# Attention values weighed in four column tiles of 32, softmax sums taken apart, x's parts in two homes

## The reference, cut to what matters

```python
q, k, v = wq @ xf, wk @ xf, wv @ xf            # 32 channels each, per image
att = softmax(einsum('bmi,bmj->bij', k, q), axis=2)
x = x + wo @ einsum('bij,bmj->bmi', att, v)    # attention 1
t = tokens(x)                                  # (4, 1024, 64)
u = layernorm(t); t = t + softmax(u @ u.T) @ u # attention 2
w = layernorm(t)                               # 8 experts, the best two by router
t = t + sum_of_two(p_k * (w @ expert_k + bias_k))
```

## Time and profile before

| | us |
|---|---|
| median of 3 executions | 223.43 (223.21 to 224.67) |
| the profiled execution's own time | 224.33 |
| its span, first to last instruction | 222.6 |
| TensorE busy | 206.3 |
| VectorE busy | 143.4 |
| ScalarE busy | 107.6 |
| GpSimd busy | 62.5 |

### The profile page before, as it was taken

One profiled execution on the slowest core, in us unless ns is written; L12 is line 12 of the kernel. 1 busy time (PEld: TensorE's weight loads), 2 busy tenths in 40 slices (PEclk: granted clock), 3 DMA queues, 4 the chain that ended last, 5 costly groups with the idle time before them and its releaser, 6 DMA issues.

```text
span 222.6 us, 2932 instructions
## 1 busy us (share of the span) xinstructions
PE 206.3 (93%) x1075; PEld 105.1 (47%) x1075; DVE 143.4 (64%) x358; ACT 107.6 (48%) x166; POOL 62.5 (28%) x75
## 2 busy tenths in 40 slices
PE   7899899969989989999999999899999999998993
PEld 2454443543643434643543445334445343477773
DVE  2589865776334898168189665836775282798970
ACT  2630664283675476564654544765645567201110
POOL 8230000044040030003001268730177751017260
PEclk9999999996999999999999999999999999999999
DMA  4661000000000000000000000020000002000021
GB/s 105 145 148 43 3 0 0 0 1 0 3 1 0 0 0 3 0 0 0 3 0 1 0 3 1 0 47 0 3 0 0 0 3 49 0 0 3 0 47 47
DMA packets 3341, 3.67 MB, mean 16 GB/s; under 512 B 2176, under 2 KB 2432, under 8 KB 3328
## 3 DMA queue, kind: packets, MB, share of 16 engines
q1 hardware_dynamic: 3328, 3.50, 6.9%
HBM read 2.45 MB, written 1.05 MB: 16 GB/s over the span
## 4 chain that ended last, share of the span: by engine, by line
PE 67%; DVE 18%; ACT 5%; POOL 4%; issue 2%; DMA 1%; SPq 1%; DVEq 0%; POOLq 0%
PE acc L490 22%; DVE rowmax L1107 7%; PE ring L551 6%; PE ring L596 6%; PE ring L552 5%; PE ring L465 4%; PE ring L483 4%; PE acc L626 3%; POOL sm L368 3%; PE ring L443 2%; PE ring L454 2%; PE ring L455 2%; PE ring L444 2%; DVE stats L1140 1%; DVE tok L1186 1%
## 5 line engine op out<-in xcount | busy, mean ns | idle before, releaser
L902 ACT ACTIVATE prob<-ring,shift 128x1024 f32<-128x1024 f32 x32 | 35.6, 1112 | 27.6 <-PE ring L552 27.5
L1107 DVE TENSOR_REDUCE rowmax<-ring 128x1 f32<-128x1024 f32 x32 | 37.9, 1219 | 15.6 <-PE ring L465 15.4
L899 ACT ACTIVATE prob<-ring 128x1024 f32<-128x1024 f32 x32 | 32.1, 1024 | 20.1 <-PE ring L483 19.9
L368 POOL TENSOR_TENSOR sm<-sm,minus_half 128x8 f32<-128x8 f32 x8 | 15.8, 1975 | 85.4 <-DVE sm L1150 85.4
L490 PE MATMUL acc<-prob,val 128*64 128x512 f32 x128 | 32.0, 622 | 0.0
L490 PE MATMUL acc<-prob,u 128*64 128x512 f32 x128 | 31.0, 606 | 0.0
L1246 DVE TENSOR_TENSOR prod<-ring,gate 128x1024 f32<-128x1024 f32 x16 | 19.4, 1221 | 9.3 <-PE ring L596 8.8
L551 PE MATMUL ring<-zst 128*128 128x512 f16 x64 | 24.5, 383 | 0.4 <-DVE rowmax L1107 0.4
L552 PE MATMUL ring<-zsw,zst 128*128 128x512 f16 x64 | 24.3, 379 | 0.0
L483 PE MATMUL ring<-kst,qst 98*128 98x512 f32 x64 | 21.4, 425 | 2.2 <-ACT prob L899 0.9
L465 PE MATMUL ring<-qst,kst 96*128 96x512 f32 x64 | 22.4, 436 | 0.6 <-DVE rowmax L1107 0.4
(11 more groups left out here) (155 smaller groups left out, 311.0 us busy)
## 6 DMA issues: line engine op xcount, KB each, us to landing
xin<-in_x SPq DMA_DIRECT2D x8, 256.0 KB, 3.9
out<-ob SPq DMA_DIRECT2D x6, 128.0 KB, 2.3
e_in<-in_L_ffn_expert_w SPq DMA_DIRECT2D x2, 128.0 KB
out<-ob SPq DMA_DIRECT2D x4, 64.0 KB, 2.0
eb_in<-in_L_ffn_expert_b SPq DMA_DIRECT2D x8, 2.0 KB
wo<-in_L_conv_wo SPq DMA_DIRECT2D x2, 8.0 KB, 2.4
r_in<-in_L_ffn_router_w SPq DMA_DIRECT2D x2, 2.0 KB
w<-in_L_conv_wq SPq DMA_DIRECT2D x1, 16.0 KB, 3.5
```

Of the source, the lines that this page charges most:

```text
L368: pool.tensor_tensor(sm[:, 3, :], sm[:, 2, :], minus_half[:, :], ALU.pow).then_inc(s_rs, 1)
L899: act.activation(prob1[:, j % DEEP, :], flat(filled(act, f"st{j}", b)), ACT.Exp).then_inc(s_p1, 1)
L902: act.activation(prob2[:, j % DEEP, :], flat(filled(act, f"s{j}", b)), ACT.Exp, bias=shift[:, :], accum_out=rsum2[b % 2][:, j:j + 1]).then ...
L1107: dve.tensor_reduce(rowmax[:, tile:tile + 1], flat(filled(dve, f"mx{tile}", b)), AX.X, ALU.max).then_inc(s_mx, 1)
```

## The change

- Values are weighed in four column tiles of 32, each with a quarter of the 1024 columns; the ones column in the stationary tile is gone, and with it the padding to 64.
- For images 0 and 1 the softmax sums are matmuls of their own: `sum1` multiplies the same `prob1` by a tile of ones, after each pair of weighings. `project_out` picks them with a small matmul.
- For images 2 and 3 ScalarE takes them: `sum_row` reads the maxima's scores in the ring buffer, once `row_max` (which now gives the negative maximum) is done, and writes their exp in place with an accumulated sum. Only then is the buffer released.
- `xst` has two homes. `round_x(2)` and `round_x(3)` move into the exps of image 0, `split_x(3)` ahead of the first `rstd`.
- Image 1's `project_v` and `values` move ahead of image 0's `max_row`; `split_k(1)` ahead of it too; the fillers of `keep_clock` there are 4 instead of 3 + 3.
- `wo4` is one load and waits for nothing. `project_out` has two matmuls over 256 columns instead of four over 130. `eb_blk` is made later.

The core of the diff (index changes of `xst` and renumbered waits are mostly left out; blank lines too):

```diff
 DEEP = 4
+QUARTER = N // 4
+BY_ROWS = (2, 3)
...
-HEAD = [("w3", 0), ("q", 0), ("k", 0), ("vx", 0)] + per_tile("mx", 0) + [("q", 1), ("k", 1), ("mr", 0)]
+HEAD = [("w3", 0), ("q", 0), ("k", 0), ("vx", 0)] + per_tile("mx", 0) + [("q", 1), ("k", 1), ("vx", 1), ("mr", 0)]
...
 FIRST = [("st0", 0), ("st1", 0), ("mx0", 1), ("st2", 0), ("mx1", 1), ("st3", 0), ("mx2", 1), ("mx3", 1), ("st4", 0),
-         ("mx4", 1), ("st5", 0), ("mx5", 1), ("st6", 0), ("mx6", 1), ("st7", 0), ("mx7", 1), ("vx", 1), ("mr", 1),
-         ("po", 0)]
+         ("mx4", 1), ("st5", 0), ("mx5", 1), ("st6", 0), ("mx6", 1), ("st7", 0), ("mx7", 1), ("mr", 1), ("po", 0)]
...
         wo4 = sb("wo4", [C, 4, M])
+        ones = sb("ones", [P, M])
...
         vx2 = sb("vx2", [P, M + C], F32R)
-        wo_blk = sb("wo_blk", [P, 2, C + 1])
+        wo_blk = sb("wo_blk", [P, 4, C])
+        pick = sb("pick", [P, 4])
...
-        xst = sb("xst", [P, N], F32R)
+        xst = two("xst", [P, N], F32R)
...
         kst = two("kst", [P, N], F32R)
-        val = two("val", [P, T, C])
+        val = two("val", [P, T, M])
...
         rinv1 = sb("rinv1", [P, T])
+        rsum1 = two("rsum1", [P, T])
...
                 return table[name]
+            if name[:-1] == "mx" and b in BY_ROWS:
+                return s_row, T * BY_ROWS.index(b) + int(name[-1]) + 1
...
                 sp.dma_start(w3[n * M:(n + 1) * M, :, :], w.unsqueeze(1).to_broadcast([M, 2, C])).then_inc(s_w3, 16)
-            sp.wait_ge(s_const, 1)
-            for h in range(2):
-                sp.dma_start(wo4[:, 2 * h, :], wo).then_inc(s_wol, 16)
+            sp.dma_start(wo4[:, :, :], wo.unsqueeze(1).to_broadcast([C, 4, M])).then_inc(s_wol, 16)
...
         def _(pool):
-            pool.memset(wo4[:, :, :], 0.0).then_inc(s_const, 1)
+            pool.memset(ones[:, :], 1.0).then_inc(s_const, 1)
...
                                pattern=[[-1, P]], channel_multiplier=1).then_inc(s_const, 1)
-            pool.memset(nmax[:, :, :].bitcast(F32), 0.0)
-            for home in range(2):
-                pool.memset(val[home][:, :, M + 1:C], 0.0)
-                pool.memset(val[home][:, :, ONE:ONE + 1], 1.0).then_inc(s_pool, 1)
+            pool.memset(nmax[:, :, :].bitcast(F32), 0.0).then_inc(s_pool, 1)
+            pool.wait_ge(s_pool, 2)
+            pool.memset(qst[0][ROW:ROW + 2, :].bitcast(F32), 1.0).then_inc(s_pool, 1)
             pool.wait_ge(s_pool, 3)
-            pool.memset(qst[0][ROW:ROW + 2, :].bitcast(F32), 1.0).then_inc(s_pool, 1)
-            pool.wait_ge(s_pool, 4)
...
             pool.wait_ge(s_const, 3)
+            pool.memset(pick[:, :], 0.0)
...
             pool.memset(tile_mask[:, :], 1.0).then_inc(s_pool, 1)
-            pool.wait_ge(s_pool, 5)
+            pool.wait_ge(s_pool, 4)
...
                                pattern=[[-E, T]], channel_multiplier=1).then_inc(s_pool, 1)
-            pool.wait_ge(s_pool, 6)
+            pool.wait_ge(s_pool, 5)
...
                 pool.wait_ge(s_xr, b + 2)
-                first = xst[C:P, :]
+                first = xst[b % 2][C:P, :]
...
             split_x(2)
+            split_x(3)
             rstd(0, s_ve1, s_rs1, sm1)
-            split_x(3)
...
                         pe.wait_ge(s_xs, h + 1)
-                    rows = xst[:, h * CHUNK:(h + 1) * CHUNK]
+                    rows = xst[b % 2][:, h * CHUNK:(h + 1) * CHUNK]
...
+            def quarter(b, j, q):
+                return prob1[:, j % DEEP, :].rearrange("p (h q n) -> p q h n", h=2, q=4)[:, q]
...
                     pe.wait_ge(s_gbs, 1)
-                weigh(acc1, val[b % 2], prob1, j, s_p1, s_av1, b)
+                pe.wait_ge(s_p1, T * b + j + 1)
+                for q in range(4):
+                    mm = pe.matmul(acc1[q * M:(q + 1) * M, 0:QUARTER], val[b % 2][:, j, :], quarter(b, j, q),
+                                   start=(j == 0), stop=(b in BY_ROWS and j == T - 1))
+                if b in BY_ROWS and j == T - 1:
+                    mm.then_inc(s_av1, 1)
+            def sum1(b, j):
+                for q in range(4):
+                    mm = pe.matmul(acc1[q * M:(q + 1) * M, QUARTER:2 * QUARTER], ones[:, :], quarter(b, j, q),
+                                   start=False, stop=(j == T - 1))
+                if j == T - 1:
+                    mm.then_inc(s_av1, 1)
...
                 weigh1(b, j + 1)
+                if b not in BY_ROWS:
+                    sum1(b, j)
+                    sum1(b, j + 1)
...
                 if b == 0:
-                    pe.wait_ge(s_wblk, 2)
-                for t in range(4):
-                    o = (t % 2) * 2 * (C + 1)
-                    mm = pe.matmul(buf[:, t // 2, o:o + 2 * (C + 1)], agg[:, t * P:(t + 1) * P],
-                                   wo_blk[:, :, :].rearrange("p h c -> p (h c)"), start=True, stop=True)
+                    pe.wait_ge(s_wblk, 4)
+                for h in range(2):
+                    mm = pe.matmul(buf[:, h, 0:4 * C], agg[:, h * P:(h + 1) * P],
+                                   wo_blk[:, :, :].rearrange("p q c -> p (q c)"), start=True, stop=True)
+                    if b not in BY_ROWS:
+                        mm = pe.matmul(buf[:, h, 4 * C:4 * C + 4], agg[:, QUARTER + h * P:QUARTER + (h + 1) * P],
+                                       pick[:, :], start=True, stop=True)
...
                     keep_clock(2)
-            pe.wait_ge(s_wol, 2 * 16)
+            pe.wait_ge(s_wol, 16)
...
             project_qk("k", 1)
-            keep_clock(3)
+            project_v(1)
             max_row(0)
-            keep_clock(3)
+            keep_clock(4)
...
             weigh_pair1(0, 6)
-            project_v(1)
...
                 act.wait_ge(s_x[b], 32)
-                act.activation(xst[:, :], xin[:, b, :], ACT.Copy).then_inc(s_xr, 1)
+                act.activation(xst[b % 2][:, :], xin[:, b, :], ACT.Copy).then_inc(s_xr, 1)
...
+            def sum_row(b, tile):
+                buf = flat(filled(act, f"mx{tile}", b))
+                act.wait_ge(s_mx, T * b + tile + 1)
+                act.activation(buf, buf, ACT.Exp, bias=rowmax[:, tile:tile + 1],
+                               accum_out=rsum1[b % 2][:, tile:tile + 1]).then_inc(s_row, 1)
...
                 act.wait_ge(s_av1, b + 1)
-                act.activation(agg[:, :], acc1[:, :], ACT.Copy).then_inc(s_agg, 1)
+                width = QUARTER if b in BY_ROWS else CHUNK
+                act.activation(agg[:, 0:width], acc1[:, 0:width], ACT.Copy).then_inc(s_agg, 1)
...
             for h in range(2):
-                act.activation(xst[:, chunk(h)], xin[:, 0, chunk(h)], ACT.Copy).then_inc(s_xr, 1)
+                act.activation(xst[0][:, chunk(h)], xin[:, 0, chunk(h)], ACT.Copy).then_inc(s_xr, 1)
...
                     act.activation(dst[0:ROW, chunk(h)], ring[0:ROW, k, h, :], ACT.Copy).then_inc(s_rounded, 1)
-            act.wait_ge(s_const, 3)
...
             round_k(1)
+            values(1)
...
-            for j in range(4):
+            for j in range(3):
                 exp1(0, j)
+            round_x(2)
+            exp1(0, 3)
...
                 act.activation(r_blk[rows, h, 0, :], r_in[rows, :], ACT.Copy).then_inc(s_er, 1)
-            for j in range(4, T):
-                exp1(0, j)
+            exp1(0, 4)
+            exp1(0, 5)
+            round_x(3)
+            exp1(0, 6)
+            exp1(0, 7)
             copy_agg(0)
-            values(1)
             max_row(1)
-            round_x(2)
...
             values(2)
-            round_x(3)
...
             exp1(1, 6)
+            sum_row(2, 0)
             exp1(1, 7)
+            sum_row(2, 1)
...
             exp2(0, 0)
+            sum_row(2, 2)
...
             exp2(0, 1)
+            sum_row(2, 3)
             exp2(0, 2)
+            sum_row(2, 4)
...
             exp2(0, 3)
+            sum_row(2, 5)
...
             exp2(0, 4)
+            sum_row(2, 6)
...
             exp2(0, 6)
+            sum_row(2, 7)
...
             max_row(2)
+            sum_row(3, 0)
...
             exp1(2, 0)
-            for j in range(1, 6):
-                exp1(2, j)
+            sum_row(3, 1)
+            exp1(2, 1)
+            exp1(2, 2)
+            sum_row(3, 2)
+            exp1(2, 3)
+            exp1(2, 4)
+            sum_row(3, 3)
+            exp1(2, 5)
...
             gap_exp(0)
 
+            sum_row(3, 4)
             exp2(1, 0)
...
             exp2(1, 1)
+            sum_row(3, 5)
...
             exp2(1, 3)
+            sum_row(3, 6)
...
             stack_swapped(2)
+            sum_row(3, 7)
...
             def row_max(b, tile):
-                dve.tensor_reduce(rowmax[:, tile:tile + 1], flat(filled(dve, f"mx{tile}", b)), AX.X, ALU.max).then_inc(s_mx, 1)
+                dve.tensor_reduce(rowmax[:, tile:tile + 1], flat(filled(dve, f"mx{tile}", b)), AX.X, ALU.max,
+                                  negate=True).then_inc(s_mx, 1)
...
                 rm = rowmax[:, :].unsqueeze(2)
```

(41 more changed lines are left out.)

9 lines of the change are left out of this document (5 added, 4 removed).

## The result

The changed kernel takes 232.78 us (median of 4 executions, 231.34 to 234.13); before, 223.55 in the same round. The ratio is 1.039, 95% interval 1.0347 to 1.0433: slower by 9.2 us. The profiled execution took 233.8 us, its span is 232.1.

What follows compares the result with a forecast made beforehand. It took TensorE, busy 206.3 of 222.6 us, as the bound. 222.6 - 4.9 - 0.9 + 7.45 + 1.55 - 1.3 made 224.5; that +1.9 on the median 223.43 gave 225.4 us, range 218.5 to 229.0.

Steps and rivals of the forecast that it cites:

- a rival of one stretch at one place, 82 to 87: TensorE idles 3.9 of 5.3 us, the clock drops, some 1.5 us of work doubled: 226.9; shared chance 0.26.
- the cost of the change to ones: Switching from values to ones in the weighings costs 0.15 us each time, giving 226.6; shared chance 0.26.
- the walk through the queues: Following the code's order with profiled durations, from 50.2 us, adding stall to stall: 224.5 in all.
- the lead of 5.8 us out of the first stage: Maxima of image 2 (mx1(2)) start at 60.5 us, 5.8 ahead of before.
- Four column tiles: Weighing in full overlap: 1.0 us a pair for images 2 and 3, 1.87 with sums for images 0 and 1.
- x in two homes: First stage: q(2) no longer waits for x(2)'s split, 4.9 us won with moved values; exp1(1,5) another 0.9.
- Values moved ahead: Image 1's values projection leaves the first stage's end, where 1.8 us goes; scores1(1,0) comes 0.9 us earlier.
- The dearest place: From 77.85 to 87.6 us, ScalarE's queue behind sum_row(2,5): a lead of 4.2 us becomes 1.65 behind.
- Image 3's sums: sum_row(3,4) and sum_row(3,5) hold exps behind them, costing 1.2 and 1.0 us; then 3.2 behind.
- The norm chain swallows the won weighing: Won 0.86 us of weigh(2,0) and (2,2), and image 3's (3,0) and (3,2), vanish in waits for VectorE and GpSimd.
- The rival of waits that catch up: From 60.5 us, VectorE and ScalarE run ahead while TensorE stands; half of 11.6 us regained: 219.6; chance 0.28.
- Four tiles not side by side: In the weighings four column tiles run two at a time, 13.8 us more: 242; chance 0.10.

Runs made afterwards that it cites:

- b_fillers: Changed kernel with 39 unused filler matmuls put where TensorE waits, the last six held until VectorE has read attention 2's result: 227.74 us, ratio 1.0176.
- f_rows_image2: Changed kernel with ScalarE row sums for image 2 alone, image 3's sums taken by ones on TensorE: 232.99 us, ratio 1.0381.
- k_tiles_only: Kernel before with only the four column tiles and sums by ones for all images; one x home, values unmoved, no row sums: 224.56 us, ratio 1.0023.
- c_two_homes: Kernel before with only xst in two homes and round_x(2) ahead of exp1(0,3): 220.85 us, ratio 0.9844.
- i_round_x3_earlier: Kernel before with xst's two homes alone, and round_x(3) ahead of values(2) instead of behind it: 220.02 us, ratio 0.9782.
- a_ones_everywhere: Changed kernel with the sums of all four images by ones on TensorE, no row sums on ScalarE: 220.84 us, ratio 0.9857.
- m_splits_later: Changed kernel with all sums by ones, VectorE's splits of experts' and router's weights moved from image 1's row maxima to behind split_k(2): 220.15 us, ratio 0.9789.
- d_order: Changed kernel with round_k(3) ahead of sum_row(2,5) and copy_high(1) ahead of sum_row(2,6) on ScalarE: 226.81 us, ratio 1.012.
- g_rows_image3: Changed kernel with ScalarE row sums for image 3 alone, image 2's sums by ones on TensorE: 223.16 us, ratio 0.9956.
- q_no_sums: Changed kernel with softmax sums of images 2 and 3 left out, 1 in their place, row_max freeing the buffer: 220.28 us, ratio 0.9806.
- e_order_fillers: Changed kernel with both ScalarE's reordering of round_k(3) and copy_high(1) and the filler matmuls in TensorE's waits: 227.52 us, ratio 1.0155.
- h_short_sums2: Changed kernel with each row sum reading one column instead of 1024 and giving 1, order and buffer release kept: 223.37 us, ratio 0.9964.

## Why the prediction was wrong

It gave 225.4, at most 229.0; 232.8 was measured, 7.4 over the forecast. The direction held; the range did not.

**The step that failed is the clock.** The sum has no term for it. The prediction had it as a rival of one stretch at one place, 82 to 87, worth 1.5 us, which shares a chance of 0.26 with the cost of the change to ones. There were three places, 13.6 us at the lower level, and b_fillers puts 5.0 us on them. The first came behind the wait of 1.75 us at 65.78, which stood in the walk through the queues: `scores1(1,7)` from 61.2, two tiles of scores, then `scores2(0,0)` at 64.15 leave some 1.6 us of waiting, with no clock price at all. The third came behind waits of 1.13 and 0.73 us. A walk that lists waits of 1.0 to 1.5 us had its candidates before it; but f_rows_image2 shows that such a wait doesn't bring the drop each time.

**A second term was mis-sized: the lead of 5.8 us out of the first stage.** `max_scores(2,1)` was to start at 60.5 and started at 62.37, a lead of some 4.0 (66.34 before). These rows are `scores1(1,0)`, before, in the changed kernel and in k_tiles_only, which leaves the values where they were:

```profile
46.52 1.74 PE L483 MATMUL ring<-kst,qst 98*128 98x512 f32 x6
```

```profile
47.27 1.90 PE L488 MATMUL ring<-kst,qst 98*128 98x512 f32 x6
```

```profile
47.17 1.90 PE L488 MATMUL ring<-kst,qst 98*128 98x512 f32 x6
```

It was to come 0.9 us earlier than before and comes 0.75 later. 0.5 of the difference is there at the stage's start (`scores1(0,0)` at 26.73, where the prediction had 26.25). With the 5.0 us of the clock this 1.9 makes 6.9 of the 7.4.

**The walk itself was near, when the clock is up.** Starts in us:

| | before | walk | b_fillers | the change |
|---|---|---|---|---|
| second `project_qk`, q(2) | 50.55 | 47.4 | 48.1 | 49.1 |
| `scores2(0,0)` | 68.38 | 64.15 | 64.8 | 65.8 |
| `u_transposed(1)` | 85.95 | 87.6 | 88.4 | 90.9 |
| `att2_transposed(0)` | 97.98 | 99.4 | 100.4 | 105.8 |
| `w_transposed(0)` | 106.15 | 108.25 | 109.2 | 114.7 |
| `w_transposed(1)` | 147.52 | 150.7 | 151.9 | 158.2 |
| span | 222.6 | 224.5 | 225.7 | 232.1 |

The change leaves the walk by 1.7 us in the first stage, by 1.7 more from the first low stretch to `u_transposed(1)`, and by 3.1 over the second low stretch; from `w_transposed(0)` on by 1.1 only. b_fillers, with the change's waits and the clock at 1.00, stays 0.7 to 1.2 us from the walk throughout. A part of that nearness is luck: its `scores1(0,0)` came at 25.74, 0.5 earlier than the walk's. And the walk's own steps from `w_transposed(0)` to 3.2 behind (2.1 behind, 1.8 given back, 1.2 and 1.0 added) add up to 2.5; the other 0.7 has no source.

Point by point:
- Four column tiles: right. 1.07 us a pair for 1.0, and 0.88 from its start to that of the sums (60.51 to 61.39) for 0.86; k_tiles_only shows nothing beside it. The estimate by the Trainium skill's page "TensorE: Matmul & The Clock Gate" (Part 3), 5 us more, did not come: the measurement decides for full overlap of four.
- x in two homes: right in kind. 4.9 + 0.9 was too much: c_two_homes wins 3.6, and with one copy earlier 4.4 to 4.9 (i_round_x3_earlier).
- Values moved ahead: wrong. The 0.9 us won at the end of the first stage was nothing. In a_ones_everywhere q(2) starts at 48.90, in c_two_homes, which leaves the values where they were, at 48.95. From `scores1(0,0)` to `scores1(1,0)` the change takes 20.5 us and k_tiles_only 21.8, but the change begins the stage 1.4 later (26.73 for 25.34). No run moves the values alone. A split of the router's weights on VectorE, 2.1 us long beside GpSimd's (see the last section), is in the way of image 1's maxima; the prediction had no term for it, and m_splits_later shows some 0.8 us.
- The dearest place: right in place, order and size. 9.8 us from `split_q(3)` to `u_transposed(1)` was the walk's number (77.85 to 87.6) and is the trace's; d_order, the experiment on it, gave 3.6 us there.
- Image 3's sums: without the 1.8 won by image 2's weighings and with the 1.3 won by its own, the prediction's terms make it 2.05 us (1.55 + 1.8 - 1.3); g_rows_image3 shows 2.3. On top of image 2's it cost nothing, which the sum didn't have.
- The norm chain swallows the won weighing: right, and more so. Some 3 us of 6.9 were to come through; q_no_sums shows about 1, and 3 at the edge.
- The rival of waits that catch up (0.28): not seen in the trace. The waits of image 2's stage stood one behind the other as in the walk. Four tiles not side by side (0.10): out. The exps in place took 1084 ns, within what the forecast assumed.

Not tried: row sums with a fourth ring buffer, and a release of the buffer ahead of the row sum, which reads it.

## What to carry to other kernels

Work that is moved off the bounding engine onto an engine with idle time is not free if it stands between two engines in a small ring: price the buffer's longer hold and the head of the in-order queue, not the share of busy time. Look first whether the shorter work is on the chain at all; here an 8 us chain of VectorE and GpSimd ran beside it. And give each new TensorE wait a second price, with a chance to it, for the work behind it at half the clock (1.75, 1.99 and 2.08 us of waiting brought it here, and 1.75 once didn't), or stand fillers in it; where the wait has gone, they only lengthen the queue (e_order_fillers).

## What the runs showed of the hardware

- Four column tiles of 32 with float32 operands and 256 columns run side by side in full: 16 records in 1.07 us, where two column tiles of 64 with 512 columns take 1.94 for 8.
- The granted clock fell behind waits of 1.75 us (the change and d_order, at 66), 1.99 (q_no_sums, at 102) and in one of 2.08 (the change, at 90). It stayed at 1.00 behind 1.75 us in f_rows_image2, with the same 2.25 us busy of the 4.00 from 62 to 66, and behind 1.65 at 105.68 in h_short_sums2. In the changed kernel it was at 1.2 GHz from 66.4 to 69.8, from 90.3 to 97.1 and from 124.4 to 127.8, and b_fillers puts 5.0 us on these 13.6.
- A VectorE instruction on 8 elements a row took 2.1 us while GpSimd's split ran, from this timeline of the changed kernel (both splits of the router's weights, 2.31 us together, the first 2.11; in m_splits_later, away from it, they took 0.16 each):

```profile
39.60 2.37 POOL L379 TENSOR_TENSOR xst<-xin,xst 64x1024 fp32r<-64x1024 f32 x1 [5.78 <-ACT xst L902]
...
39.88 2.31 DVE L1356 TENSOR_TENSOR r_blk<-r_in,r_blk 64x8 fp32r<-64x8 f32 x2
```

The long one ends with GpSimd's, at 41.97 (0.02 us later). The Trainium skill's page "GPSIMD Engine Reference" (1. Specifications) says that GpSimd's SBUF interfaces are shared with VectorE, with contention where a VectorE instruction has two SBUF inputs; this one has. The maxima, which read PSUM, kept their time beside GpSimd's earlier split (31.43 to 33.82): three in 3.49 us from 31.84.
